# A graph attention layer on one Trainium2 core: its preparation rearranged, R copied through HBM, plain fp32 in five of eight projections

## Chip, core and metric

One of the eight cores of a Trainium2 chip. The metric is the device time of one execution in microseconds (us).

## What is computed

x is 4096 x 256 in fp32, adj a 4096 x 4096 matrix of 0 and 1 (int32), W1 is 256 x 256.

```python
h0 = jnp.maximum(_layernorm(x, axis=-1), 0.0)
h = h0 @ W1 + b1
e = jax.nn.leaky_relu((h @ a1)[:, None] + (h @ a2)[None, :] + b2, 0.2)
attention = jnp.where(adj > 0, e, jnp.float32(-1000000000000.0))
attention = jax.nn.softmax(attention, axis=1)
x = x + jax.nn.elu(attention @ h)
```

## The kernel before

The work has a preparation and a main loop. The engines have streams written out by hand, with semaphores between them; an instruction that waits holds all that stands behind it on its engine.

**Preparation.** The 32 tiles of 128 nodes go in 8 groups of 4. For a group g:

- `statistics` (VectorE): four `bn_stats`. `moments` (GpSimd): seven small steps that make mean and variance of them. `root` (ScalarE): square root. `invert` (VectorE): reciprocal and shift. `normalise`: two tiles by ScalarE, two by VectorE, into `xn`.
- `transposes` (TensorE): eight of 128 x 128 into PSUM. `relu_T` (ScalarE): relu of these into `hnT`, with row sums. `low_T` (VectorE): what the rounding to fp32r lost, into `hnT_lo`.
- `project` (TensorE): four tiles times two halves of the features, each as three fp32r matmuls (`hnT` by `W_hi`, `hnT` by `W_lo`, `hnT_lo` by `W_hi`), 258 columns. The last two columns give the two scores, h a2 and a multiple of h a1. `keep_h` (VectorE) adds the bias and writes `h_raw`, in two halves (L700).
- `exponents` (GpSimd) makes `cr`, `s2` and `cp` of the two scores. The row scores have to stand along the free dimension in every partition, as `R` (128 x 4096): `repeat_s1` (ScalarE), four transposes in `spread` (TensorE), `keep_s` (ScalarE, L374), and an exp over 1,024 columns for each chunk of rows (L378).

At the end come the sum of all h (L568, with which `h_tiny` is made), the maximum over `s2` by way of a transpose and a small matmul (L573, L575), `u` (L428), the first `hp_hi` and `hp_lo`, that is h times u in two parts.

**Main loop.** 4 chunks of 1,024 rows, in each 16 pairs of column tiles, in 4 rounds of 4 slots. For a pair: a DMA of 1 MB of adj; `sign` (ScalarE, L383); `mask` (VectorE, two instructions, L738): the larger of R and p, times the sign; `high` (ScalarE, L391) rounds to `w_hi`; `low` (VectorE, L748) writes the rest, `w_lo`; TensorE multiplies `w_hi` by `hp_hi` and `hp_lo` (32 matmuls of 258 columns, L604 and L606) and `w_lo` by `hp_hi` (16, L604) into 8 banks. In chunk 0, `scale_h`, `round_h` and `low_h` make the h of the next pairs beside that. `start_sum` puts a matmul with `h_tiny` (L580) into each bank at a chunk's start. After a chunk, ScalarE copies the banks to `y` (L455).

## Time and profile before

| | |
|---|---|
| median of 3 runs | 437.5 us (437.46 to 437.55) |
| profiled execution, its own time | 437.48 us |
| its span, first to last instruction | 435.7 us |
| TensorE busy | 412.5 us |
| VectorE busy | 377.1 us |
| ScalarE busy | 315.9 us |
| GpSimd busy | 23.0 us |
| read from HBM | 76.15 MB |

A span is shorter than the execution's own time by what lies before the first and after the last instruction. An engine counts as busy from the start of an instruction to its end, and instructions on one engine overlap a little, so that the step from one to the next is shorter than the duration of one. Each start that is named in the text is in us from the span's start.

### The profile page before, as it was taken

The page shows a single profiled execution, that of the slowest core. Times are in us where ns is not written, and L with a number is a line of the kernel's source. Part 1 is how long each engine was busy: PE and PEld are TensorE (multiplying, and loading weights), DVE is VectorE, ACT ScalarE, POOL GpSimd, SP SyncE. Part 2 cuts the span into 40 slices and gives each one's busy share as a digit, 9 for nine tenths or more (in the row PEclk, how much of TensorE's full clock was granted, in tenths as well). Part 3 has the DMA queues.
Part 4 walks back from the last instruction along what each step waited for, and adds up shares of the span by engine and source line. Part 5 has one row for each costly group of instructions (what it writes and reads, how often), then busy time and mean ns, then how long its engine had stood idle before and what let it go on. Part 6 is the DMA issues. An engine that isn't in the chain of part 4 may idle for free.

```text
span 435.7 us, 8648 instructions
## 1 busy us (share of the span) xinstructions
PE 412.5 (95%) x3399; PEld 409.1 (94%) x3399; DVE 377.1 (87%) x404; ACT 315.9 (73%) x312; POOL 23.0 (5%) x94
## 2 busy tenths in 40 slices
PE   0689979999999999999999999999999999999995
PEld 0688979999999999999999999999999999999995
DVE  3999899999999389999996299999991799999925
ACT  2678899999996298957763798859562989586512
POOL 2333200000000000000000000000000000000003
PEclk9999999999999999999999999999999999999999
DMA  8940015556555725638478155647477256476202
GB/s 271 385 178 1 0 45 211 193 213 211 193 193 194 289 93 205 235 145 261 173 254 308 68 193 200 249 152 263 154 265 259 73 219 213 174 243 238 98 0 98
DMA packets 22360, 80.68 MB, mean 185 GB/s; under 512 B 1472, under 2 KB 14016, under 8 KB 14144
## 3 DMA queue, kind: packets, MB, share of 16 engines
q1 hardware_dynamic: 21920, 79.70, 52.1%
q10 hardware_dynamic: 416, 0.66, 0.5%
q8 instruction: 16, 0.26, 0.2%
q14 instruction: 8, 0.07, 0.0%
HBM read 76.15 MB, written 4.19 MB: 184 GB/s over the span
## 4 chain that ended last, share of the span: by engine, by line
PE 88%; DVE 7%; ACT 2%; DMA 2%; issue 0%; SPq 0%; DVEq 0%; ACTq 0%
PE ps L604 51%; PE ps L606 25%; PE ps L622 2%; PE ps L623 2%; PE ps L624 2%; DVE stats L664 2%; DMA x_s<-x 2%; DVE hnT_lo L691 1%; PE ps L531 1%; DVE h_raw L700 1%; PE ps L533 1%; PE ps L532 1%; DVE xn L681 1%; PE ps L580 1%; PE ps L519 1%; ACT h_raw L439 1%
## 5 line engine op out<-in xcount | busy, mean ns | idle before, releaser
L604 PE MATMUL ps<-hp_hi,w_hi 128*128 (+1 forms) x944 | 229.8, 282 | 0.9 <-ACT w_hi L391 0.9
L606 PE MATMUL ps<-hp_lo,w_hi 128*128 (+1 forms) x944 | 229.7, 282 | 0.0
L738 DVE SCALAR_TENSOR_TENSOR adj_s<-R,p,adj_s 128x1024 f32<-128x1024 f32 x128 | 158.1, 1275 | 31.7 <-ACT adj_s L383 31.7
L604 PEld LDWEIGHTS ps<-hp_hi,w_hi 128*128 128x128 f32 x944 | 178.3, 189 | 1.2 <-ACT w_hi L391 1.1
L606 PEld LDWEIGHTS ps<-hp_lo,w_hi 128*128 128x128 f32 x944 | 178.1, 189 | 0.0
L748 DVE SCALAR_TENSOR_TENSOR w_lo<-adj_s,w_hi 128x2048 fp32r<-128x2048 f32 x64 | 146.0, 2282 | 0.4 <-ACT w_hi L391 0.3
L391 ACT ACTIVATE w_hi<-adj_s 128x2048 fp32r<-128x2048 f32 x64 | 122.4, 1912 | 29.8 <-DVE adj_s L738 29.5
L383 ACT ACTIVATE adj_s<-adj_s 128x2048 f32<-128x2048 int32 x64 | 122.3, 1912 | 23.2 <-DMA adj_s<-adj_t 23.0
L604 PE MATMUL ps<-hp_hi,w_lo 128*128 (+1 forms) x944 | 123.1, 283 | 0.6 <-DVE w_lo L748 0.6
L604 PEld LDWEIGHTS ps<-hp_hi,w_lo 128*128 128x128 f32 x944 | 117.4, 189 | 0.8 <-DVE w_lo L748 0.8
L455 ACT ACTIVATE y<-ps 128x258 f32<-128x258 f32 x24 | 9.3, 387 | 27.9 <-PE ps L624 27.9
L330 POOL TENSOR_TENSOR adj_s<-y,adj_s 128x256 f32<-128x256 f32 x7 | 4.8, 692 | 372.9 <-DVE y L886 372.9
L519 PE MATMUL ps<-ident,xn 128*128 128x128 f32 x64 | 10.2, 312 | 15.1 <-ACT xn L350 11.3
L519 PEld LDWEIGHTS ps<-ident,xn 128*128 128x128 f32 x64 | 8.5, 161 | 15.8 <-issue 11.5
L622 PE MATMUL ps<-hp_hi,w_hi 128*128 128x258 f32 x80 | 22.6, 282 | 0.0
L623 PE MATMUL ps<-hp_lo,w_hi 128*128 128x258 f32 x80 | 22.6, 282 | 0.0
L624 PE MATMUL ps<-hp_hi,w_lo 128*128 128x258 f32 x80 | 22.5, 282 | 0.0
L531 PE MATMUL ps<-W_hi,hnT 128*128 128x258 f32 x64 | 19.1, 299 | 0.8 <-DVE h_raw L700 0.6
L532 PE MATMUL ps<-W_lo,hnT 128*128 128x258 f32 x64 | 18.3, 287 | 0.0
L533 PE MATMUL ps<-W_hi,hnT_lo 128*128 128x258 f32 x64 | 18.3, 286 | 0.0
L664 DVE BATCH_NORM_STATS2 stats<-x_s 128x6 f32<-128x256 f32 x32 | 11.2, 411 | 6.0 <-DMA x_s<-x 6.0
L623 PEld LDWEIGHTS ps<-hp_lo,w_hi 128*128 128x128 f32 x80 | 15.1, 189 | 0.0
(90 smaller groups left out, 270.2 us busy)
## 6 DMA issues: line engine op xcount, KB each, us to landing
adj_s<-adj_t SPq DMA_DIRECT2D x64, 1024.0 KB, 4.8
x_s<-x SPq DMA_DIRECT2D x8, 512.0 KB, 10.4
o_s<-x SPq DMA_DIRECT2D x3, 1024.0 KB, 7.5
out<-o_s SPq DMA_DIRECT2D x6, 512.0 KB, 6.8
adj_s<-x SPq DMA_DIRECT2D x1, 1024.0 KB, 5.3
out<-adj_s SPq DMA_DIRECT2D x8, 128.0 KB, 1.7
vec<-vectors ACTq DMA_DIRECT2D x1, 384.5 KB, 6.4
W1x<-W ACTq DMA_DIRECT2D x1, 256.0 KB, 4.3
```

The lines of the kernel that those rows point to most:

```text
L383: act.activation(adj_w[:, c, :, :], adj_s[:, c, :, :], ACT.Sign).then_inc(signed, 1)
L391: act.activation(w_hi[:, c, :, :], adj_w[:, c, :, :], ACT.Relu).then_inc(hi_ready, 1)
L519: last = pe.transpose(ps[:, kc, t * P:(t + 1) * P], xn[:, u, t, kc * P:(kc + 1) * P], ident[:, :])
L531: pe.matmul(acc, hnT[:, u, kc, node], W_hi[:, kc, :], start=kc == 0, stop=False)
L532: pe.matmul(acc, hnT[:, u, kc, node], W_lo[:, kc, :], start=False, stop=False)
L604: last = pe.matmul(acc, block_w, hh, start=False, stop=False)
L606: pe.matmul(acc, block_w, hl, start=False, stop=False)
L622: pe.matmul(acc, w_hi[:, b + k, s, col], hh, start=False, stop=False)
L623: pe.matmul(acc, w_hi[:, b + k, s, col], hl, start=False, stop=False)
L624: last = pe.matmul(acc, w_lo[:, b + k, s, col], hh, start=False, stop=end)
L738: last = dve.scalar_tensor_tensor(sgn, R[:, ds(ic * CW, CW)], p[:, ds(source(r, c) + s, 1)], sgn, ALU.max, ALU.mult)
L748: dve.scalar_tensor_tensor(w_lo[:, c, :, :], adj_w[:, c, :, :], 0.0, w_hi[:, c, :, :].bitcast(fp32), ALU.max, ALU.subtract).then_inc(lo_re ...
```

## The change

- Mean and variance come from `bn_aggr` on VectorE, 32 of them; GpSimd's `moments` is gone.
- W and the vectors are loaded by the queue of x, after group 0; the first tile of adj after all of x.
- ScalarE normalises three tiles of a group from group 2 on, VectorE one. `xn` has four buffers, and the transposes take turns between two pairs of banks.
- Groups 0 to 4 are projected by plain fp32 matmuls (8 a group, no `low_T`); groups 5 to 7 as before by three products (24).
- 19 matmuls on ones stand at the start of TensorE's stream (`keep_warm`).
- `R`: `turn_r` transposes `cr` in one piece (first 8 tiles, then 24), VectorE copies it, ScalarE takes exp of the compact rows, SyncE writes them to HBM and reads them back spread over all partitions.
- The steps after the last projection take `s2` and `cr` straight from PSUM, ahead of the last `keep_h`. The matmuls with `h_tiny` move from a chunk's start to its last pair. The sum of h stands inside the last projection.
- In the first pair, `low` stands ahead of the next pair's `mask`.

```diff
-NORM_ACT = 2
+NORM_ACT = 3
+PAIRED = 2
+WARM = 19
+XN = 4
+SPLIT = 5
+R_CUT = CW // P
+R_PART = ((0, R_CUT), (R_CUT, TILES))
-EARLY = 6 * GT
+EARLY = 4 * GT
...
+            load_nodes(0)
+            sp.dma_start(W1x[:, :, 0:F], W1.rearrange("(c p) f -> p c f", p=P)).then_inc(w_in, 16)
+            sp.dma_start(vec[:, :], vectors.partition_broadcast(P)).then_inc(vec_in, 16)
+            for g in range(1, GROUPS):
                 load_nodes(g)
...
+            def spread(k):
+
+                a, b = R_PART[k]
+                tiles = slice(a, b)
+                sp.wait_ge(r_ready, k + 1)
+                sp.dma_start(r_rows[tiles, :], r_row[k][:, :]).then_inc(r_out, 16)
+                sp.wait_ge(r_out, (k + 1) * 16)
+                sp.dma_start(R[:, a * P:b * P],
+                             r_rows[tiles, :].rearrange("t p -> (t p)").partition_broadcast(P)).then_inc(R_in, 16)
...
+            def exp_r(k):
+
+                act.wait_ge(r_copied, k + 1)
+                act.activation(r_row[k][:, :], r_row[k][:, :], ACT.Exp).then_inc(r_ready, 1)
...
+            def keep_warm(n):
+
+                for _ in range(n):
+                    pe.matmul(ps[:, H0 + GT - 1, 0:P], ones[:, :], ones[:, :], start=True, stop=True)
...
+                        if g < SPLIT:
+                            last = pe.matmul(acc, hnT[:, g % 2, kc, node], W1x[:, kc, :], start=kc == 0, stop=kc == KC - 1)
+                        else:
+                            pe.matmul(acc, hnT_hi[:, g % 2, kc, node], W_hi[:, kc, :], start=kc == 0, stop=False)
+                            pe.matmul(acc, hnT_hi[:, g % 2, kc, node], W_lo[:, kc, :], start=False, stop=False)
+                            last = pe.matmul(acc, hnT_lo[kc][:, g % 2, node], W_hi[:, kc, :], start=False, stop=kc == KC - 1)
...
+            keep_warm(WARM)
             pe.wait_ge(pool_c, 3)
...
+            transposes(0)
+            pe.wait_ge(w1x_ready, 1)
+            project(0)
+            transposes(1)
+            project(1)
+            transposes(2)
+            project(2)
+            transposes(3)
+            for g in range(3, GROUPS):
+                if g + 1 < GROUPS:
+                    transposes(g + 1)
+                if g == 4:
+                    pe.wait_ge(c_ready, R_CUT // GT)
+                    pe.wait_ge(hn_ready, (g + 1) * KC)
+                    turn_r(0)
+                project(g)
+                if g == 4:
+                    pe.wait_ge(r_copied, 1)
...
                 for ib in range(BANKS):
                     acc = ps[:, ib, 0:HW].unsqueeze(1)
                     col = slice(ib * P, (ib + 1) * P)
+                    add_tiny(ib)
...
-                last.then_inc(stat_ready, 1)
+                link(last)
+                for t in range(GT):
+                    dve.bn_aggr(agg[:, g, t, :], stats[:, g, t, :]).then_inc(agg_ready, 1)
...
                 for c in range(SLOTS):
                     end = last and r is LAST_ROUND
-                    if not (end and c == SLOTS - 1):
+                    begin = first and r is FIRST_ROUND and c == 0
+                    if not (end and c == SLOTS - 1) and not begin:
                         mask(*ahead(ic, r, c, 1))
                     low(ic, r, c)
+                    if begin:
+                        mask(*ahead(ic, r, c, 1))
```

VectorE's stream around the first mask (adj_s<-R,p,adj_s) before. hnT_lo is the low part of a group, here of group 7; h_raw is what `keep_h` writes, ahead of the mask for group 6 and behind it for group 7.

```order
L691 SCALAR_TENSOR_TENSOR hnT_lo<-ps,hnT 128x512 [waits hn_ready,h_ready]
L691 SCALAR_TENSOR_TENSOR hnT_lo<-ps,hnT 128x512 [waits hn_ready]
L700 TENSOR_TENSOR h_raw<-ps,b1x 128x516 [waits h_ready] x2
L782 TENSOR_REDUCE hsum<-hs 128x2 [waits hn_ready]
L784 TENSOR_SCALAR hsrep<-ones,hsum 128x128 [waits dve_c]
L784 TENSOR_SCALAR hsrep<-ones,hsum 128x128
L738 SCALAR_TENSOR_TENSOR adj_s<-R,p,adj_s 128x1024 [waits signed,R_ready,p_ready]
L738 SCALAR_TENSOR_TENSOR adj_s<-R,p,adj_s 128x1024
L700 TENSOR_TENSOR h_raw<-ps,b1x 128x516 [waits h_ready] x2
```

The same place in the changed kernel; the first two rows are the low part of group 6, R_in is the semaphore of the DMA that brings R.

```order
L708 SCALAR_TENSOR_TENSOR hnT_lo_54<-ps,hnT_hi 128x512 [waits hn_ready,h_ready]
L708 SCALAR_TENSOR_TENSOR hnT_lo_55<-ps,hnT_hi 128x512 [waits hn_ready]
L754 SCALAR_TENSOR_TENSOR adj_s<-R,p,adj_s 128x1024 [waits signed,R_in,p_ready]
L754 SCALAR_TENSOR_TENSOR adj_s<-R,p,adj_s 128x1024
L721 TENSOR_TENSOR h_raw<-ps,b1x 128x516 [waits h_ready] x2
L708 SCALAR_TENSOR_TENSOR hnT_lo_54<-ps,hnT_hi 128x512 [waits hn_ready,h_ready]
L708 SCALAR_TENSOR_TENSOR hnT_lo_55<-ps,hnT_hi 128x512 [waits hn_ready]
```

The mask moved ahead of the `h_raw` of group 6 and of the low part of group 7, and waits for a DMA instead of for ScalarE.

VectorE's stream in the changed kernel from the last `h_raw` of the preparation into the first pairs.

```order
L721 TENSOR_TENSOR h_raw<-ps,b1x 128x516 [waits h_ready] x2
L834 MEMSET h_raw 128x4 [waits h_kept]
L835 MEMSET h_raw 128x4
L905 SCALAR_TENSOR_TENSOR hp_lo<-h_raw,u,hp_hi 128x258 [waits hp_tile] x2
L764 SCALAR_TENSOR_TENSOR w_lo<-adj_s,w_hi 128x2048 [waits hi_ready]
L754 SCALAR_TENSOR_TENSOR adj_s<-R,p,adj_s 128x1024 [waits signed]
L754 SCALAR_TENSOR_TENSOR adj_s<-R,p,adj_s 128x1024
L870 TENSOR_TENSOR hp_lo<-h_raw,hp_hi 128x516 [waits hp_pair]
```

Before, the two rows of the mask (of pair 1) stood ahead of `w_lo` (of pair 0), directly behind `hp_lo`.

ScalarE's stream in the changed kernel around the exp of r (r_row<-r_row), from the relu of group 6 on.

```order
L366 ACTIVATE hnT_hi,hs<-ps 128x512 [waits tp_ready,h_ready]
L366 ACTIVATE hnT_hi,hs<-ps 128x512 [waits tp_ready]
L372 ACT_TABLE_LOAD
L372 ACTIVATE r_row<-r_row 8x128 [waits r_copied]
L413 ACTIVATE p<-cp 128x16 [waits c_ready]
L366 ACTIVATE hnT_hi,hs<-ps 128x512 [waits tp_ready,h_ready]
```

The compact exp over 8 rows stands where the exp over 1,024 columns of R (L378) and two copies to R stood.

## Rows read from the trace of the kernel before

**Rows 1.** The page: busy us of each engine, share of the span, instructions.

```profile
PE 412.5 (95%) x3399; PEld 409.1 (94%) x3399; DVE 377.1 (87%) x404; ACT 315.9 (73%) x312; POOL 23.0 (5%) x94
```

**Rows 2.** Windows: length; busy PE, PEld, DVE, ACT, POOL; granted clock; DMA share; GB/s.

```profile
0.00:57.70 57.70, 40.40 (x301) 37.58 (x302) 46.96 (x135) 38.15 (x82) 18.17 (x87) 1.00 0.44 158
65.68:429.00 363.32, 363.32 (x3031) 363.32 (x3032) 319.07 (x254) 268.72 (x217) 2.76 (x4) 1.00 0.55 194
```

**Rows 3.** Waits of TensorE from 50 us on: us in total, times, longest.

```profile
PE ps L604 <- ACT w_hi L391: 0.9, 1, 0.9
...
PE ps L604 <- DVE w_lo L748: 0.6, 1, 0.6
```

**Rows 4.** The chain that ended last, 50 to 66 us: start, us, what.

```profile
50.91 2.39 DVE adj_s L738 x2
53.30 1.22 DVE h_raw L700 x2
...
56.13 0.33 ACT u L428
...
56.54 0.91 ACT hp_hi L433 x2
...
63.82 1.81 ACT w_hi L391
...
65.68 0.39 PE ps L604
```

**Rows 5.** Timeline of the first group: start, us of all in the row, instruction.

```profile
5.32 1.41 DVE L664 BATCH_NORM_STATS2 stats<-x_s 128x6 f32<-128x256 f32 x4 [4.37 <-DMA x_s<-x]
...
8.18 0.20 POOL L308 TENSOR_TENSOR var<-mom 128x4 f32<-128x4 f32 x1
...
9.70 0.16 DVE L671 RECIPROCAL rstd<-std 128x4 f32<-128x4 f32 x1
...
12.35 0.21 DVE L715 TENSOR_SCALAR W1x<-w1a 128x1 f32<-128x1 f32 x2
```

**Rows 6.** Timeline of TensorE: start, us of all in the row, instruction.

```profile
11.35 1.94 PE L519 MATMUL ps<-ident,xn 128*128 128x128 f32 x8 [11.35 <-ACT xn L350]
...
17.79 0.42 PE L531 MATMUL ps<-W_hi,hnT 128*128 128x258 f32 x1
...
18.52 0.28 PE L532 MATMUL ps<-W_lo,hnT 128*128 128x258 f32 x1
...
22.32 1.07 PE L519 MATMUL ps<-ident,xn 128*128 128x128 f32 x8 [1.59 <-DVE xn L681]
...
52.62 0.28 PE L533 MATMUL ps<-W_hi,hnT_lo 128*128 128x258 f32 x1
52.74 1.03 PE L568 MATMUL ps<-W1x,hsrep 128*128 128x256 f32 x4
```

**Rows 7.** Groups of instructions: busy us, mean ns of one, idle before. ACT_TABLE_LOAD likewise.

```profile
L691 DVE SCALAR_TENSOR_TENSOR hnT_lo<-ps,hnT 128x512 fp32r<-128x512 f32 x16 | 10.3, 684 | 1.8 <-ACT hnT L360 1.8
...
L360 ACT ACTIVATE hnT<-ps 128x512 fp32r<-128x512 f32 x16 | 9.3, 589 | 5.1 <-PE ps L519 5.1
...
L748 DVE SCALAR_TENSOR_TENSOR w_lo<-adj_s,w_hi 128x2048 fp32r<-128x2048 f32 x2 | 4.6, 2286 | 0.1
...
L415 ACT ACT_TABLE_LOAD x1 | 1.3, 1283 | 0.0
...
L568 PE MATMUL ps<-W1x,hsrep 128*128 128x256 f32 x4 | 1.0, 379 | 0.0
...
L455 ACT ACTIVATE y<-ps 128x258 f32<-128x258 f32 x24 | 9.3, 387 | 27.9 <-PE ps L624 27.9
```

**Rows 8.** DMA issues: number, KB each, median us to landing; x_s alone last.

```profile
adj_s<-adj_t SPq DMA_DIRECT2D x64, 1024.0 KB, 4.8
...
out<-adj_s SPq DMA_DIRECT2D x8, 128.0 KB, 1.7
...
DMA to landing us min/median/max: 4.6/10.4/12.6
```

More of the change, by code:

```diff
@@ L534, in project @@
                     if t % (GT // 2) == GT // 2 - 1:
                         last.then_inc(h_ready, 1)
-            def spread(g, u):
-                pe.wait_ge(s1_ready, g + 1)
-                if at_least(g, 2):
-                    pe.wait_ge(s_kept, g - 1)
-                for t in range(GT):
-                    last = pe.transpose(ps[:, S0 + u, t * P:(t + 1) * P], s1rep[:, u, t, :], ident[:, :])
-                last.then_inc(s_ready, 1)
-            pe.wait_ge(pool_c, 3)
-            transposes(0, 0)
@@ L564, in _, with turn_r @@
-            project(GROUPS - 1, 1)
-            pe.wait_ge(hsrep_ready, 1)
-            for kc in range(KC):
-                last = pe.matmul(ps[:, 0, 0:F], hsrep[:, kc, :], W1x[:, kc, 0:F], start=kc == 0, stop=kc == KC - 1)
-            last.then_inc(hsum_ps, 1)
-            spread(GROUPS - 2, 0)
+                    if g == GROUPS - 1 and t == 1:
+                        sum_h()
+            def turn_r(k):
+                a, b = R_PART[k]
+                pe.transpose(ps[0:b - a, RB[k], 0:P], cr[:, a:b], ident[:, :]).then_inc(rT_ready, 1)
@@ new lines, in add_tiny, with first_tile @@
+            def add_tiny(ib):
+                pe.matmul(ps[:, ib, 0:HW], ones64[:, :], h_tiny[:, :], start=False, stop=False)
+            def first_tile():
+                pe.wait_ge(hi_ready, 1)
+                pe.wait_ge(hp_tile, 1)
+                pe.wait_ge(hsum_kept, 1)
+                pe.wait_ge(r_copied, 2)
+                for ib in range(BANKS):
+                    if ib == H0:
+                        pe.wait_ge(h_kept, 2 * GROUPS)
+                    pe.matmul(ps[:, ib, 0:HW], w_hi[:, 0, 0, ib * P:(ib + 1) * P], hp_hi[:, 0, :], start=True, stop=False)
+                pe.wait_ge(hp_first, 1)
+                for ib in range(BANKS):
+                    pe.matmul(ps[:, ib, 0:HW], w_hi[:, 0, 0, ib * P:(ib + 1) * P], hp_lo[:, 0, :], start=False, stop=False)
@@ L587, in pair @@
                     for s in range(2):
+                        if first and begin and part == 0 and s == 0:
+                            first_tile()
+                            continue
                         if first and part == 0:
@@ L637, in chunk @@
                 last_pairs(ic, PAIRS - tail, SLOTS - tail, first, tail)
-            pe.wait_ge(prep_done, 1)
-            for ib in range(S0):
-                start_sum(ib)
             chunk(0, first=True)
@@ new lines, in _ @@
+            keep_h(0)
+            invert(2)
+            normalise(2)
+            statistics(3)
+            invert(3)
+            normalise(3)
+            keep_h(1)
+            statistics(4)
+            invert(4)
+            normalise(4)
+            scalars()
+            for g in range(2, GROUPS - 1):
+                if g + 3 < GROUPS:
+                    statistics(g + 3)
+                keep_h(g, (0,))
+                if g + 3 < GROUPS:
+                    invert(g + 3)
+                    normalise(g + 3)
+                if g == 4:
+                    copy_r(0)
+                if g == SPLIT - 2:
+                    split_weights()
+                keep_h(g, (1,))
+                if g + 1 >= SPLIT:
+                    low_T(g + 1)
+                if g == 5:
@@ L804, in _ @@
-            rest = slice(P // 2, P)
-            dve.wait_ge(tiny_ready, 1)
-            dve.scalar_tensor_tensor(h_tiny[rest, :], h_sum[rest, :], TINY, h_tiny[rest, :].bitcast(fp32),
-                                     ALU.mult, ALU.subtract).then_inc(prep_done, 1)
+            dve.wait_ge(hn_ready, GROUPS * KC)
+            link(dve.reduce_sum(hsum[:, :], hs[:, :, :], AX.X))
+            for kc in range(KC):
+                last = dve.tensor_scalar(hsrep[:, kc, :], ones[:, :], hsum[:, kc:kc + 1], None, ALU.mult)
```

329 lines of the change are left out of this document (144 added, 185 removed).

## Prediction

> **What bounds the kernel now.** I read the page's line of busy times first: TensorE works 95% of the span [rows 1]. Windows then split the span into two stages. From 65.68 us to 429 us TensorE is busy in every microsecond, 3,031 matmuls in 363.3 us, 0.12 us each; in the first 57.7 us it works only 40.4, and VectorE with 47.0 is the busiest [rows 2]. The waits of TensorE after 50 us are 0.9 us for `w_hi` and 0.6 us for `w_lo` in the first two pairs, and nothing later [rows 3]. So the main loop is full, and its length is fixed by its matmuls; the preparation and the first pair decide. I fix one point: the matmuls on `w_hi` of pair 1 begin at 65.68 [rows 4]. From there to the end 435.7 − 65.7 = 370.0 us pass, with no wait that an earlier delivery could shorten. The question is when that point comes in the changed kernel; call it X.
>
> The chain of work back from X [rows 4]: `w_hi` of pair 1 (ScalarE, 1.8), a queue of ScalarE work back to `u` at 56.1, the maximum over `s`, the last two `h_raw`, the first mask (2.4), and TensorE's last projection, whose last matmul starts at 52.62 and ends at 52.9 [rows 6]. Call this end E: X − E is 12.8 us before. Ahead of E, VectorE and TensorE set the pace.
>
> **The main loop.** The eight matmuls with `h_tiny` per chunk stay eight. In chunk 0 they stood before X and now stand in its last pair, behind X: 8 × 0.12 = **+0.96 us**. In the later chunks they move from the first pair to the last; a bank of the first pair now lasts 0.24 instead of 0.36 us, but seven of the eight banks are copied while the last pair runs (ScalarE waits 27.9 us in all for these banks [rows 7]), so I count nothing; without that cover a copy of 0.39 would show at each of three changes of chunk. The exp of R leaves ScalarE, which waits there already: nothing.
>
> **From E to X.** Small steps follow E: copy of `s`, maximum, transpose, maximum, matmul, copy. The same steps fill 54.5 (end of `h_raw`) to 56.1 (`u`) before, 1.6 us, and the copy is one more [rows 4]. They no longer wait for `h_raw`, which now stands behind them on VectorE: E + 1.7, then 1.3 for two `h_raw`, 0.2 for the memsets and 0.8 for two `hp_lo` (as ScalarE's `hp_hi` of the same size, 0.91) gives E + 4.0; `u` and `hp_hi`, 1.2 together on ScalarE, hide beside that. Then the new order on VectorE: first `w_lo` of pair 0 (2.2), only then the mask of pair 1 (2.4), and ScalarE's `w_hi` behind it (1.8 plus 0.1 of handing over) [rows 4, 7]. X = E + 4.0 + 2.2 + 2.4 + 2.0 = E + 10.6. Before it was 12.8, so this part gives **−2.2 us**, the moved 0.96 takes part of it back, and the change breaks even if E comes not later than 52.9 + 1.25 = 54.2.
>
> **The first group.** Its statistics end in 0.3 us on VectorE where GpSimd took 1.6 (6.7 to 8.4) [rows 5], and x is alone ahead in its queue. It lands at 5.3 now, beside W and the vectors. 128 KB take 1.7 us and 1,024 KB take 4.8 [rows 8]; the straight line gives 3.0 for 512 KB, thus 3.7 after the issue at 0.7 (5.3 less the 4.6 that this load took). I take 4.3 between 3.7 and 5.3. Then 1.4 statistics, 0.5 aggregates, 0.4 root, 0.4 inverse and shift, 1.1 for two tiles on ScalarE: transposes begin at 8.0 instead of 11.35 [rows 6]. This lead of 3.3 us is what the rest can lose.
>
> **bn_aggr** is in no row, 32 of it. The nearest rows are two tensor_scalar on one column, 0.21 together (0.06 from one to the next), and a reciprocal on four, 0.16 alone [rows 5]. I take 0.09 to the next, nearer the pipelined row; at 0.06 the sum falls by 0.6, at 0.17 it rises by 1.2.
>
> **Projection in plain fp32.** L568 is a plain matmul of 256 columns; the program has two, the trace four records, spread over 1.03 us with a last one of 0.38: 0.217 from one to the next, 0.43 a matmul [rows 6, 7]. A group has eight: 3.46 us. The split form has 24 at 0.12: 2.88. So TensorE pays 0.58 more in each of five groups, and VectorE is spared 2 × 0.6 for `hnT_lo` in each [rows 7]. The chain relu, low part, matmul also loses one link. The Trainium skill (FP8 and Floating Point Precision, TensorE Precision Notes) says true fp32 takes four passes through the array, thus 4 × 0.12 = 0.48 where the row gives 0.43. By the page the sum would be 0.9 higher, and I keep the row.
>
> **Group by group, up to E.** `transposes(g+1)` stands behind `project(g)` for the first groups, so TensorE, ScalarE and TensorE follow one another. A turn is: eight transposes 0.9 (eight take 1.07 with the last one's end [rows 6]), two relus of which 1.1 lies behind them (0.59 each [rows 7]), projection 3.5. Transposes 8.0, projection 0 at 10.1 to 13.5, projection 1 at 15.6 to 19.1. Root 3 stands on ScalarE behind relu 2 (end 21.0), and VectorE, done with statistics 3 at 18.1, stands waiting for it with `h_raw` of group 1 queued behind; it comes at 22.5, and projection 2 needs that bank: 22.6 to 26.1. Projection 3 waits for `h_raw` of group 2, which stands behind statistics 5: 29.5 to 33.0. Projection 4 runs 34.0 to 37.5. Then TensorE waits for the copy of r, queued behind root 8 and normalise 7: 39.1. Transposes 6, the low part of group 5 (1.3), and projection 5 is 40.9 to 43.9; transposes 7, low part 6 behind two `h_raw`, projection 6 from 46.0 to 48.9. TensorE is idle for some 12 us of this, so the saved work on VectorE turns into waits, and the lead of 3.3 is used up at about here.
>
> **R by DMA.** ScalarE gives 16 steps away (eight s1rep, eight copies to R, over 512 columns like the relu, 0.6 each), TensorE 32 transposes. In their place r goes to HBM and comes back. ScalarE finishes relu 6 at 41.3, loads the table (1.28 [rows 7]) and takes exp: 42.7. The write is 4 KB: 1.3 by the line, 1.7 as for 128 KB, 3.0 if it costs what 512 KB cost; I take 1.75, by the nearest row. The read of 512 KB: 3.0 by the line, 4.6 as the quickest x [rows 8]; nothing else is under way, so nearer the line, 3.4. R lands at 42.7 + 1.75 + 3.4 = 47.9. VectorE has been waiting with the first mask since 45.9, and **behind it stand `h_raw` 6 and the low part of group 7**, on which the last projection hangs. Mask 2.4, h_raw 1.2, low part 1.3: 52.8. Projection 7 with the sum of h inside it: 24 × 0.12 + 2 × 0.43 = 3.75, and its tail 0.25: **E = 56.8**.
>
> **Sum.** X = 56.8 + 10.6 = 67.4. Span = 67.4 + 370.0 + 0.96 = 438.4, against 435.7: **+2.7 us**. The profiled execution took 437.48, 1.8 more than its span and as long as the median of 437.5. Forecast: 437.5 + 2.7 = **440.2 us**, slower by 0.6%. A change under 0.2%, 0.9 us, cannot be told from none.
>
> **The rivals.**
> *R is there in time* (chance 0.12). The two transfers take under 3.2 us together and the mask does not wait. E falls by up to 2.0 and the time to 438.2 to 438.9: within or just beyond what can be told. Against it: no transfer in the profile lands in under 1.7, and half a megabyte has taken 4.6 at the least.
>
> *The lead holds* (faster; chance 0.08). It decides on TensorE between 8.0 and E. Its work there is 8 × 0.9 + 5 × 3.46 + 3 × 2.88 + 0.86 = 34.0 us, so that 14.8 us of the 48.8 are waits. If these waits are 3.6 us shorter, E comes before 53.2 and the kernel is faster; if the lead of 3.3 stays whole, E is 49.6 and the time 433.0 us. For it speaks that 6.5 us of `hnT_lo` and a quarter of the normalising leave VectorE, the bound of that stage. Against it: the order of the code puts a wait for another engine into each turn.
>
> *The clock falls* (chance 0.22). TensorE's eight transposes take 1.94 us at 11.35 and 1.07 at 22.3, and a matmul lasts 0.42 at 17.8 and 0.28 at 18.5 [rows 6]: 1.2 GHz, then 2.4, though the granted clock reads 1.00 [rows 2]. It rose under steady work, after two bursts of transposes. Nineteen plain matmuls on 128 columns now come first, 0.22 each at the upper level (half of 0.43) and 0.43 at the lower: 4 to 8 us from 0.95 on. I take 7.2 and a raised clock at 8.0; all at the lower level would put the transposes at 9.2. But for R TensorE stands idle from 48.9 to 52.8, longer than the 1.6 ahead of 22.3, which the upper level outlasted. Projection 7 at the lower level costs 2.9 to 3.7 more: 443 to 444 us. Lost already in group 0 and 1, it costs 1.5 to 3.5: 442 to 444. The Trainium skill (TensorE: Matmul & The Clock Gate, Why this matters for your kernels) also warns that idle gaps between matmul bursts bring the lower clock back; no row here shows a fall.
>
> **How the numbers follow.** The sum as it stands, 0.58: its bounds are −0.6 and +1.0 for x, −0.6 and +1.2 for bn_aggr, −0.8 and +2.5 for R; not all at one end they make 439.0 to 442.2. With R in time 438.2, with a lost clock 444. Leaving out the lead and the worst of the clock, the range is 438.3 to 444.0. Slower by over 0.2%: 0.58 + 0.22 + a part of R in time = 0.82; same 0.10; faster 0.08.
>
> **What would show it.** Right: transposes near 8.0; plain matmuls in two records of 0.22; a wait of VectorE on the DMA of R ahead of the first mask, about 2 us, and one of TensorE of nearly 4 us ahead of the last projection; E near 56.8; about 2 us of waiting for `w_hi` of pair 1, at 67.4; no wait later. Wrong: transposes after 9; E before 54; R landed before the mask; matmuls 0.24 apart after 8 us; TensorE waiting in the later rounds or where chunks meet.

## The result and the profile after

The changed kernel takes 442.86 us (median of 4 runs, 441.27 to 444.19), against 437.52 us (437.46 to 437.68, 4 runs) on the same chip: ratio 1.012, 95% interval 1.010 to 1.0139. It is slower by 5.3 us; 440.2 was forecast. The profiled execution is the quickest of the four, 441.27 us with a span of 439.3, at a mean granted clock of 0.995. The other three have 0.991 and take 1.3 to 2.9 us more: times that agreed to 0.2 us before now scatter over 2.9.

The page of the changed kernel has, for busy times, the line that answers to [rows 1].

```profile
PE 417.3 (95%) x3367; PEld 411.4 (94%) x3367; DVE 372.4 (85%) x423; ACT 308.8 (70%) x300; POOL 10.6 (2%) x39
```

VectorE, ScalarE and GpSimd all work less than before, and the kernel is longer. Windows show where (columns as in [rows 2]); the last is the stretch from the start of `w_hi` of pair 1, the point X, to 432 us.

```profile
41.50:46.50 5.00, 4.52 (x25) 4.55 (x26) 0.92 (x2) 2.38 (x7) 0.00 (x0) 0.66 0.07 27
46.50:68.50 22.00, 14.85 (x113) 13.59 (x111) 17.43 (x33) 13.88 (x22) 1.51 (x7) 1.00 0.35 132
68.50:432.00 363.50, 363.49 (x3034) 363.49 (x3035) 320.14 (x256) 266.70 (x213) 2.75 (x4) 1.00 0.55 193
```

From X on TensorE is full as before. Ahead of it TensorE stands idle for 7.15 of the 22 us, and in the window of 41.5 the granted clock reads 0.66. TensorE's waits of the whole execution (us in total, times, longest):

```profile
PE ps L532 <- DVE hnT_lo L708: 4.4, 3, 2.2
PE ps L530 <- DVE h_raw L721: 3.7, 2, 2.6
PE ps L530 <- DVE W1x L736: 1.8, 1, 1.8
PE ps L621 <- ACT w_hi L385: 1.6, 1, 1.6
PE ps L594 <- ACT hp_hi L424: 1.4, 1, 1.4
PE ps L514 <- DVE r_row L771: 1.2, 1, 1.2
```

TensorE's timeline (start, us of all in the row, in brackets the idle time ahead and its releaser) has the preparation, with projections 0, 2 and 3 in plain fp32:

```profile
1.00 6.27 PE L503 MATMUL ps<-ones 128*128 128x128 f32 x38 [1.00 <-POOL ones L312]
8.11 1.07 PE L514 MATMUL ps<-ident,xn 128*128 128x128 f32 x8 [0.84 <-ACT xn L356]
10.96 3.75 PE L530 MATMUL ps<-W1x,hnT 128*128 128x258 f32 x16 [1.79 <-DVE W1x L736]
...
23.78 3.73 PE L530 MATMUL ps<-W1x,hnT 128*128 128x258 f32 x16 [2.59 <-DVE h_raw L721]
...
30.61 3.73 PE L530 MATMUL ps<-W1x,hnT 128*128 128x258 f32 x16 [1.14 <-DVE h_raw L721]
...
41.98 0.36 PE L532 MATMUL ps<-W_hi,hnT_hi 128*128 128x258 f32 x1 [0.90 <-DVE hnT_lo L708]
...
42.30 0.42 PE L534 MATMUL ps<-W_hi,hnT_lo 128*128 128x258 f32 x1
42.52 0.42 PE L532 MATMUL ps<-W_hi,hnT_hi 128*128 128x258 f32 x1
...
48.80 0.35 PE L532 MATMUL ps<-W_hi,hnT_hi 128*128 128x258 f32 x1 [1.30 <-DVE hnT_lo L708]
...
54.11 0.36 PE L532 MATMUL ps<-W_hi,hnT_hi 128*128 128x258 f32 x1 [2.18 <-DVE hnT_lo L708]
```

The first transposes are at the upper level and at the time forecast (8.0). Projection 0 waits for `W1x`, which waits for the vectors. Inside projection 5 the matmuls go over from 0.12 to 0.215 us apart and last 0.42 each, as in the row at 17.79 of [rows 6]: 1.2 GHz, until 45.7.

VectorE's timeline says why TensorE waits:

```profile
5.70 0.38 DVE L683 BATCH_NORM_AGGREGATE agg<-stats 128x2 f32<-128x6 f32 x4
...
22.33 0.18 DVE L689 RECIPROCAL rstd<-std 128x4 f32<-128x4 f32 x1 [3.08 <-ACT std L347]
...
22.95 1.28 DVE L721 TENSOR_TENSOR h_raw<-ps,b1x 128x516 f32<-128x516 f32 x2
...
47.27 1.28 DVE L708 SCALAR_TENSOR_TENSOR hnT_lo<-ps,hnT_hi 128x512 fp32r<-128x512 f32 x2
48.50 2.48 DVE L754 SCALAR_TENSOR_TENSOR adj_s<-R,p,adj_s 128x1024 f32<-128x1024 f32 x2
50.89 0.69 DVE L721 TENSOR_TENSOR h_raw<-ps,b1x 128x516 f32<-128x516 f32 x1
51.97 0.69 DVE L721 TENSOR_TENSOR h_raw<-ps,b1x 128x516 f32<-128x516 f32 x1 [0.38 <-PE ps L534]
52.58 1.28 DVE L708 SCALAR_TENSOR_TENSOR hnT_lo<-ps,hnT_hi 128x512 fp32r<-128x512 f32 x2
```

VectorE stands idle 3.08 us for the root of group 3, with `h_raw` of group 1 ready to be written behind it, and projection 2 hangs on that. And between 48.50 and 53.8 it works through mask, two `h_raw` and the low part of group 7, in this order, while TensorE waits for the last of them. It stands idle for 0.38 us of this, ahead of the second `h_raw`, until projection 6 has ended. No bracket stands at the mask: in this execution R was there in time. The chain that ended last (start, us, what) has R and the way to X:

```profile
43.83 1.22 DMA r_rows<-r_row
45.07 2.88 DMA R<-r_rows
...
58.14 0.16 DVE s L821
...
59.82 0.33 ACT u L419
60.24 0.91 ACT hp_hi L424 x2
...
66.61 1.86 ACT w_hi L385
68.52 0.39 PE ps L621
```

The chain's 2.88 for the read of R ends at 47.95, where the chain goes on with a low part of VectorE; it isn't the transfer's own length. From issue to landing the list of DMA issues has 3.3 us:

```profile
R<-r_rows SPq DMA_DIRECT2D x1, 512.0 KB, 3.3
```

So R lands at 45.07 + 3.3 = 48.4, 0.1 us before the mask starts. The last projection ends at 58.1 (E), and X is 68.52: X − E is 10.4.

### The profile page after: what moved, and what is told of

Same layout as the page of the kernel before. It is cut to its first block, busy times and chain, and to the rows that moved or that the text cites. A ratio compares the mean times of both kernels' runs of the same rounds, so it can differ in the third digit from the quotient of the medians.

```text
span 439.3 us, 8507 instructions
## 1 busy us (share of the span) xinstructions
PE 417.3 (95%) x3367; PEld 411.4 (94%) x3367; DVE 372.4 (85%) x423; ACT 308.8 (70%) x300; POOL 10.6 (2%) x39
## 4 chain that ended last, share of the span: by engine, by line
PE 87%; ACT 5%; DVE 4%; DMA 3%; issue 1%; SPq 0%; ACTq 0%; DVEq 0%
PE ps L621 51%; PE ps L623 25%; PE ps L643 2%; PE ps L641 2%; PE ps L642 2%; PE ps L530 2%; DMA vec<-vectors 2%; DVE stats L680 1%; PE ps L583 1%; ACT adj_s L377 1%; DVE h_raw L721 1%; DMA R<-r_rows 1%; ACT hnT L366 1%; ACT h_raw L430 1%; PE ps L532 1%
## 5 line engine op out<-in xcount | busy, mean ns | idle before, releaser
L621 PE MATMUL ps<-hp_hi,w_hi 128*128 (+1 forms) x936 | 226.8, 282 | 1.6 <-ACT w_hi L385 1.6
L623 PE MATMUL ps<-hp_lo,w_hi 128*128 (+1 forms) x936 | 226.8, 282 | 0.0
L621 PEld LDWEIGHTS ps<-hp_hi,w_hi 128*128 128x128 f32 x936 | 176.8, 189 | 1.8 <-ACT w_hi L385 1.8
L764 DVE SCALAR_TENSOR_TENSOR w_lo<-adj_s,w_hi 128x2048 fp32r<-128x2048 f32 x64 | 146.1, 2284 | 0.0
L621 PEld LDWEIGHTS ps<-hp_hi,w_lo 128*128 128x128 f32 x944 | 117.3, 189 | 0.0
L530 PE MATMUL ps<-W1x,hnT 128*128 128x258 f32 x80 | 18.6, 385 | 6.4 <-DVE h_raw L721 3.7
L530 PEld LDWEIGHTS ps<-W1x,hnT 128*128 128x128 f32 x80 | 14.8, 189 | 9.4 <-issue 4.2
L641 PEld LDWEIGHTS ps<-hp_hi,w_hi 128*128 128x128 f32 x80 | 15.1, 189 | 0.0
L643 PEld LDWEIGHTS ps<-hp_hi,w_lo 128*128 128x128 f32 x80 | 15.0, 188 | 0.0
L496 ACT ACTIVATE y<-ps,rden 128x256 f32<-128x256 f32 x8 | 3.8, 476 | 15.4 <-DVE rden L917 15.4
L721 DVE TENSOR_TENSOR h_raw<-ps,b1x 128x516 f32<-128x516 f32 x16 | 10.6, 680 | 4.6 <-PE ps L534 4.6
L356 ACT ACTIVATE xn<-x_s,shift,rstd 128x256 f32<-128x256 f32 x22 | 11.7, 591 | 3.9 <-DVE shift L690 3.9
```

What stands on the lines that cost most here:

```text
L356: last = act.activation(xn[:, g % XN, t, :], x_s[:, tile, :], ACT.Identity, scale=rstd[:, tile:tile + 1], bias=shift[:, tile:tile + 1])
L530: last = pe.matmul(acc, hnT[:, g % 2, kc, node], W1x[:, kc, :], start=kc == 0, stop=kc == KC - 1)
L621: last = pe.matmul(acc, block_w, hh, start=fresh, stop=False)
L623: pe.matmul(acc, block_w, hl, start=False, stop=False)
L641: pe.matmul(acc, w_hi[:, b + k, s, col], hh, start=False, stop=False)
L643: last = pe.matmul(acc, w_lo[:, b + k, s, col], hh, start=False, stop=end)
```

## The experiments

Each is the changed kernel with one edit, unless it says otherwise, and its ratio is to the kernel before on the same chip (437.44 to 437.57 us). The changed kernel has 1.012 (1.010 to 1.0139), from four executions that scatter by 2.9 us. A variant whose interval overlaps this one isn't told from it by its median; there only the traces speak, and each of them shows one execution.

### Is it the clock, and the idle time before it?

Three kernels touch what TensorE does while it would stand idle. The first puts matmuls on ones into the pauses behind the transposes of group 2, behind projection 4 and ahead of projections 5 to 7; of its edit, the last three are shown.

```diff
+            def fill(bank, count):
+                for _ in range(count):
+                    pe.matmul(ps[:, bank, 0:P], ones[:, :], ones[:, :], start=True, stop=True)
...
+                if g >= SPLIT:
+                    pe.wait_ge(h_kept, 2 * g - 1)
+                    fill(H0, (4, 5, 8)[g - SPLIT])
```

> The changed kernel with plain 128-column matmuls on ones put into TensorE's pauses: 9 behind the transposes of group 2, 5 behind projection 4, and 4, 5 and 8 ahead of projections 5, 6 and 7; nothing else is changed. Theory (the time above the sum of 440.2, and the scatter of 441.3 to 444.2 from run to run, are falls of TensorE's clock in the pauses of the preparation; the profiled run had one, from 42.3 to 45.7 us): no matmul between 8 and 430 us is at 0.22, projection 5 takes 2.9 instead of 4.5 us, the median falls by 1.5 to 3 us to 440 to 441.3, and the runs lie within 0.5 us of each other. Rival (the scatter comes from DMA landings or from somewhere later, the fall costs nothing since ScalarE and the round trip of R set the pace there): the median stays within 0.8 us of 442.9 and the scatter stays; or it rises by up to 2 us, as the added matmuls stand in the way.

Measured: 441.35 us (440.63 to 445.61, 6 runs), ratio 1.0109 (1.0077 to 1.0141). In its trace projections 5 to 7 run 0.12 apart throughout. The low level comes later, in the first pair of the main loop (61.4 to 64.6), where TensorE's slower work takes the place of a wait for `w_hi` that it has otherwise. The run with the highest granted clock, 0.999, took 440.63, and the one with the lowest, 0.987, 445.61. Here the times go with the clock, which makes it the likely cause of the scatter. But the theory asked for no fall and for runs within 0.5 us, and they lie 5.0 apart; the median is 1.5 lower, which the intervals don't tell from nothing. What the clock costs the changed kernel isn't settled by this. The run at 0.999, with hardly a fall, is still 3.2 us slower than the kernel before. And now VectorE's timeline shows the wait for R (here the mask is L764):

```profile
48.28 2.48 DVE L764 SCALAR_TENSOR_TENSOR adj_s<-R,p,adj_s 128x1024 f32<-128x1024 f32 x2 [1.52 <-issue]
```

The view names no releaser. But the read of R was issued at 44.78 and took 3.4 us to land, thus 48.2, and in all six variants that show such a wait the mask starts about 0.1 us behind R's landing. The mask begins at 48.28 in place of 48.50. The fall in projection 5 of the changed kernel cost it little by itself: it lay beside the wait for R, and hid it.

The second takes the warming away.

```diff
-WARM = 19
+WARM = 0
```

> The changed kernel without the 19 matmuls on ones. Theory (they put TensorE at the upper level before group 0): transposes of group 0 take 1.94 us and projection 0 runs at 0.43 a record for at least its first 3 us; projection 0 ends 1.5 to 3.5 us later, all of it stays in the chain of the preparation, time 1.5 to 3.5 us more. Rival (W1x comes at 10.9 anyway, and the level rises within projection 0): under 1 us.

Measured: 445.05 us (443.86 to 445.95, 5 runs), ratio 1.0166 (1.0152 to 1.018), 2.2 us more than with it. TensorE's timeline:

```profile
8.32 1.94 PE L514 MATMUL ps<-ident,xn 128*128 128x128 f32 x8 [8.32 <-ACT xn L356]
11.13 5.72 PE L530 MATMUL ps<-W1x,hnT 128*128 128x258 f32 x16 [0.87 <-ACT hnT L366]
...
56.47 0.55 PE L532 MATMUL ps<-W_hi,hnT_hi 128*128 128x258 f32 x1 [3.37 <-DVE hnT_lo L708]
```

Transposes 0 take 1.94 and projection 0 takes 5.72 instead of 3.75: the warming pays in this kernel, as the theory had it. The third puts the same 19 matmuls at the start of the kernel before, and changes nothing else there.

```diff
+            for _ in range(19):
+                pe.matmul(ps[:, H0 + GT - 1, 0:P], ones[:, :], ones[:, :], start=True, stop=True)
```

> The kernel before with the 19 matmuls on ones at the start of TensorE's stream and nothing else. Theory (before the change VectorE sets the pace of the preparation, so a faster TensorE in the first groups is worth little): transposes and projection 0 at the upper level, the median within 0.6 us of 437.5. Rival (the clock is worth what it is in the changed kernel): 1 us or more faster.

Measured: 437.54 us (437.42 to 437.58 in 11 of 12 runs; the twelfth took 2,299.23 us, which nothing here explains, and is left out of the ratio), ratio 0.9999 (0.9991 to 1.0008). Its transposes of group 0 are no faster than in [rows 6]:

```profile
0.98 7.45 PE L548 MATMUL ps<-ones 128*128 128x128 f32 x38 [0.98 <-POOL ones L285]
11.33 1.94 PE L519 MATMUL ps<-ident,xn 128*128 128x128 f32 x8 [2.90 <-ACT xn L350]
```

The pause of 2.90 us behind the warming has lost the upper level again (the granted clock is 0.93 from 8 to 11 us and 0.50 from 11 to 14); in the changed kernel it is 0.84, and the level holds. The time is as forecast, but the theory isn't tested by it: its transposes and the start of projection 0 never ran at the upper level.

### What is late: R, the mask, or the low part?

The mask one group later, so that `h_raw` 6 and the low part of group 7 don't stand behind it:

```diff
-                if g == 5:
+                if g == 6:
                     dve.wait_ge(p_ready, 1)
                     dve.wait_ge(R_in, 16)
                     mask(0, 0, 0)
```

> The changed kernel with the first mask moved on VectorE behind the low part of group 7 and the h_raw of group 6. Theory (the first mask, 2.4 us, stands in the chain of the last projection, with or without a wait for R): projection 7 starts right behind projection 6, its last matmul ends about 2.2 us earlier (55.9 instead of 58.1 in the profile), and as the first w_hi (51 to 53) still comes long before it is needed, the time falls by 1.5 to 2.3 us. Rival (the first pair needs the mask early, so that the delay of w_hi takes back what the projection wins; or ScalarE is late with relu 7): the time falls by less than 0.7 us. The scatter from the clock stays in both.

Measured: 442.11 us (441.2 to 446.04, 6 runs), ratio 1.0138 (1.0105 to 1.0171). The gain of 1.5 to 2.3 us did not come. The low part of group 7 still stands behind both `h_raw` of group 6 and runs at 51.12, and TensorE's wait for it remains as it was: projection 7 starts 5.31 us after projection 6 here (52.65 against 47.34) and in the changed kernel's trace (54.11 against 48.80). So in that trace the mask delayed nothing; it filled time in which the second `h_raw` would have waited for projection 6. The mask now stands ahead of the sum of h, for which TensorE waits inside the last projection.

```profile
PE ps L532 <- DVE hnT_lo L708: 4.4, 3, 2.2
PE ps L530 <- DVE h_raw L721: 2.6, 1, 2.6
...
PE ps L549 <- DVE hsrep L813: 1.1, 1, 1.1
```

With the mask in its place and projection 5 at the upper level, it does delay: in the run of the section on the first pair, projection 7 starts 6.47 us after projection 6 (53.66 against 47.19), 1.2 later, and then runs at the lower level.

The low part is now to go ahead of both `h_raw`, and the mask behind the sum of h:

```diff
-                keep_h(g, (0,))
+                if g >= SPLIT:
+                    low_T(g + 1)
+                else:
+                    keep_h(g, (0,))
...
-                if g == 5:
-                    dve.wait_ge(p_ready, 1)
-                    dve.wait_ge(R_in, 16)
-                    mask(0, 0, 0)
...
             last.then_inc(hsrep_ready, 1)
+            dve.wait_ge(p_ready, 1)
+            dve.wait_ge(R_in, 16)
+            mask(0, 0, 0)
```

> The changed kernel with VectorE's order of the kernel before for groups 5 to 7: the low part of group g+1 ahead of both h_raw of group g, and the first mask behind the replicated sum of h, so ahead of nothing that projection 7 needs. Theory (VectorE's order costs more than the DMA of R: TensorE waits 0.9, 1.3 and 2.2 us ahead of projections 5, 6 and 7 for the low part, which stands behind h_raw and the mask): the waits ahead of 6 and 7 vanish, with about 1 us more from projection 5's follow-on, the last projection ends 4 to 5 us earlier (near 53.5 instead of 58.1) and the median falls by 4 to 5.5 us to 437.4 to 438.9. Rival (TensorE's clock decides, the pauses only move): the time falls by under 2.5 us. Second rival (R by DMA decides): the mask waits for R at 47.9 to 48, ends at 50.4, so w_hi of pair 0 is there at 52.4 and costs nothing; if it costs, the wait ahead of the first main matmul is longer than the 1.4 us of now.

Measured: **436.27 us** (435.99 to 436.71, 7 runs), ratio 0.9971 (0.996 to 0.9982), 6.6 us below the changed kernel. VectorE's timeline of this kernel:

```profile
46.68 1.29 DVE L708 SCALAR_TENSOR_TENSOR hnT_lo<-ps,hnT_hi 128x512 fp32r<-128x512 f32 x2 [0.59 <-ACT hnT_hi L366]
47.89 0.68 DVE L721 TENSOR_TENSOR h_raw<-ps,b1x 128x516 f32<-128x516 f32 x1
...
50.37 2.47 DVE L754 SCALAR_TENSOR_TENSOR adj_s<-R,p,adj_s 128x1024 f32<-128x1024 f32 x2
```

The low part of group 7 runs at 46.68 instead of 52.58. No wait of TensorE is left between projections 5 and 7, E is 53.1, and the mask finds R there: its read was issued at 45.30 and took 4.0 us, and the mask begins 1.1 us after it landed. The scatter is down to 0.7 us. The gain is above the 4 to 5.5 us of the theory. By the two traces E comes 5.0 us earlier: 3.5 are the waits ahead of projections 6 and 7, which are gone, and 1.5 the fall of the clock in projection 5, which didn't come. The edit moves two things, and as the mask alone brought nothing clear of the noise, the waits go to the low part behind `h_raw`; the low part alone wasn't run. Projection 2 ran at the lower level in this execution, 5.41 us instead of 3.73, behind the same pause of 2.59. Most of this was made good by the wait of 1.14 us ahead of projection 3, which was gone: from the start of projection 2 to that of projection 4 it is 11.83 us instead of 11.38.

### The first pair

`low` of pair 0 behind the mask of pair 1 again, as before the change:

```diff
-                    if not (end and c == SLOTS - 1) and not begin:
+                    if not (end and c == SLOTS - 1):
                         mask(*ahead(ic, r, c, 1))
                     low(ic, r, c)
-                    if begin:
-                        mask(*ahead(ic, r, c, 1))
```

> The changed kernel with the order of the kernel before in the first pair: the mask of pair 1 ahead of the low part of pair 0. Theory A, as in the prediction (w_hi of pair 1 waits for the mask behind w_lo): the wait of 1.6 us for w_hi of pair 1 shrinks by 1 us or more and the time falls by 1 us. Theory B, from the profile of the changed kernel (ScalarE is busy without a gap from 59.8 until w_hi of pair 1 starts at 66.55, so the mask that ends at 66.5 is late by nothing): the start of w_hi stays, w_lo of pair 0 comes 2.4 us later, TensorE waits before it instead, in sum less than 0.3 us either way.

Measured: 442.59 us (441.86 to 443.09, 4 runs), ratio 1.012 (1.0105 to 1.0134), no different from the changed kernel. The wait for `w_hi` of pair 1 is gone, and one of the same length for `w_lo` of pair 0 is there, as theory B had it. The 3.3 us are the wait ahead of projection 7, where VectorE's mask had waited 1.59 us:

```profile
PE ps L532 <- DVE hnT_lo L708: 5.5, 3, 3.3
...
PE ps L621 <- DVE w_lo L764: 1.6, 1, 1.6
```

### The front

W and the vectors by ScalarE's queue, instead of behind x of group 0 in SyncE's:

```diff
-            sp.dma_start(W1x[:, :, 0:F], W1.rearrange("(c p) f -> p c f", p=P)).then_inc(w_in, 16)
-            sp.dma_start(vec[:, :], vectors.partition_broadcast(P)).then_inc(vec_in, 16)
...
+            act.dma_start(W1x[:, :, 0:F], W1.rearrange("(c p) f -> p c f", p=P)).then_inc(w_in, 16)
+            act.dma_start(vec[:, :], vectors.partition_broadcast(P)).then_inc(vec_in, 16)
```

> The changed kernel with W and the vectors loaded by ScalarE's queue again, as before the change. Theory (projection 0 waited 1.8 us for W1x because the vectors landed only at 8.9 behind W in one queue, and this shifts the whole preparation): W1x is ready 1.0 to 1.3 us earlier, but x lands at 5.3 instead of 4.3 and the transposes start 1 us later; projection 0 starts at about 11.0 to 11.3 as now, time within 0.6 us of the changed kernel. Rival (one of the two loads alone is what counts): if W1x alone counts, 0.9 to 1.2 us faster; if x alone counts, 1.0 us slower.

Measured: 444.33 us (442.96 to 447.05, 5 runs), ratio 1.0152 (1.0139 to 1.0165), 1.5 us worse by the medians, more than the theory's 0.6 and with intervals that just touch. The profiled execution is the slowest of the five, 447.05, so its falls aren't those of the median. In it the transposes of group 0 begin at 9.38 behind a pause of 2.47 us, and projection 0 then takes 6.77 us, at the lower level for most of it. x of group 0 now lands at 5.53 instead of 4.26, and the vectors are ready only 0.25 us earlier (8.72 against 8.97). Projection 0 starts at 11.46 instead of 10.96. In trying to save the 0.9 us that `W1x` costs, x was made late, and in this execution the clock was lost.

Two swaps at the place where VectorE waits 3.08 us for the root:

```diff
             statistics(3)
+            keep_h(1)
             invert(3)
             normalise(3)
-            keep_h(1)
...
-            relu_T(2)
             root(3)
+            relu_T(2)
             normalise(3)
```

> Two places of the changed kernel are swapped and nothing else: VectorE writes h_raw of group 1 ahead of the inverse and shift of group 3, and ScalarE takes the root of group 3 ahead of the relu of group 2. Theory A (order): the 2.59 us that TensorE waits ahead of projection 2 come from h_raw of group 1, which stands on VectorE behind the inverse of group 3, which waits 3.08 us for the root, which stands behind relu 2. Then that wait shrinks from 2.59 to under 0.8, projection 2 begins near 22, R and the last projections come some 2 us earlier, and the time is 440.4 us (439.5 to 441.5) against 442.9. Theory B (data): the later stages are set by something else, above all by the low part of group 7 behind h_raw of group 6 and by the clock in projections 5 to 7; then the wait ahead of projection 2 shrinks but the ones ahead of projections 6 and 7 grow, and the time stays at 442 to 443.

Measured: 439.9 us (438.39 to 442.77, 7 runs), ratio 1.0059 (1.0038 to 1.008): 3.0 us below the changed kernel. This is within theory A. The profiled execution, though, is one of the two longest (442.70): in it projection 0 ran at the lower level, 5.44 us instead of 3.75, behind waits of only 1.16 and 1.30 us. Projection 2 starts behind 0.98 us of waiting instead of 2.59, projection 3 behind 0.41 instead of 1.14. The mask still stands ahead of the low part and waits 1.69 us for R, and TensorE waits 3.45 us ahead of projection 7, which then runs at the lower level. So the trace shows the waits in front go, and what theory B says of the later ones as well; no trace shows one of the executions near 439.9.

```profile
29.30 3.73 PE L530 MATMUL ps<-W1x,hnT 128*128 128x258 f32 x16 [0.41 <-DVE h_raw L721]
...
52.66 0.55 PE L532 MATMUL ps<-W_hi,hnT_hi 128*128 128x258 f32 x1 [3.45 <-DVE hnT_lo L708]
```

Both together, the low part first and the two swaps:

> The two swaps at the front (h_raw of group 1 ahead of the inverse of group 3, root of group 3 ahead of relu of group 2) together with the order of the run before (low part of the next group ahead of both h_raw for groups 5 to 7, first mask behind the sum of h), which alone measured 436.27. Theory A (both lie on one path, one after the other): the last projection ends 1 to 2.6 us earlier again, near 51.5, and the time is 434.5 us (433.8 to 435.6), below both kernels. Theory B (ScalarE is the bound by now): w_hi of pair 1 stands on ScalarE behind its own queue, and the copy of r and root 8 keep their places, so that what is gained in front turns into waits ahead of the transposes of group 6 or for w_hi; the time is 435.8 to 436.4.

Measured: **433.25 us** (433.16 to 434.32, 5 runs), ratio 0.9908 (0.9896 to 0.9921). This is below both kernels, and below theory A's range: 4.3 us below the one before, 9.6 below the changed one. TensorE's timeline (the last row is the last matmul of projection 7):

```profile
21.72 3.75 PE L530 MATMUL ps<-W1x,hnT 128*128 128x258 f32 x16 [0.98 <-ACT hnT L366]
...
27.64 3.73 PE L530 MATMUL ps<-W1x,hnT 128*128 128x258 f32 x16 [0.41 <-DVE h_raw L721]
...
37.11 1.09 PE L514 MATMUL ps<-ident,xn 128*128 128x128 f32 x8 [1.27 <-DVE r_row L771]
...
49.68 0.28 PE L534 MATMUL ps<-W_hi,hnT_lo 128*128 128x258 f32 x1
```

E is 49.96. On top of it, VectorE's copy of r ahead of the statistics of group 7, to take away the 1.27 ahead of the transposes of group 6:

```diff
             for g in range(2, GROUPS - 1):
+                if g == 4:
+                    copy_r(0)
                 if g + 3 < GROUPS:
                     statistics(g + 3)
...
-                if g == 4:
-                    copy_r(0)
```

> As the run with both changes of order, and VectorE's first copy of r stands ahead of the statistics of group 7 instead of behind the normalising of that group. If the wait of 1.2 to 1.6 us ahead of the transposes of group 6 (TensorE waits for the copy of r, which stands behind normalise 7) lies on the path, it goes and the time falls by another 0.2 to 1.2 us below that run (433.3 to 434.3 if that one takes 434.5). If the wait only moves, to the low part or the xn of group 7 which come later by the copy, nothing changes within 0.2%.

Measured: 434.81 us (432.91 to 436.42, 6 runs), ratio 0.9931 (0.9909 to 0.9953). The wait moves: nothing ahead of the transposes, 2.21 us ahead of projection 5, for ScalarE's relu. By the medians this is worse than the version before it, but in the profiled execution `W1x` came later (a wait of 2.29 instead of 1.27) and projection 0 ran at the lower level; the run with granted clock 0.999 is the quickest seen here, 432.91. That the copy of r gains nothing, or up to 0.3 us, is all that it shows.

### Is splitting the last three groups worth it?

All eight groups in plain fp32, once in the changed kernel and once in the best version:

```diff
-SPLIT = 5
+SPLIT = 8
```

> The changed kernel with all eight projections in plain fp32 (the boundary 5 moved to 8); W is still split, but not used. Theory (a plain projection costs TensorE 0.58 us more, but the wait for the low part, 4.4 us in sum, goes; the first mask stays in front of h_raw 6, which projection 7 waits for): projections 5 to 7 take 3.5 us each, one wait of 2.5 to 3 us remains ahead of projection 7, and the time falls by 0.3 to 1.2 us. Rival (plain fp32 costs what its passes cost, 3 x 0.58): 1.7 us slower. Rival (TensorE works more densely, so the clock falls less): over 1.5 us faster and less scatter.

> The version with both changes of order (433.25 us), with groups 5 to 7 in plain fp32 as well, so that no low part is left. Theory A (TensorE sets the pace of these groups once the order is right: it waits only 0.9 us ahead of projection 5 and not at all ahead of 6 and 7): three projections cost 0.58 us more each, the wait of 0.9 goes, and the time rises by 0.8 to 1.7 us to 434.1 to 435.0. Theory B (VectorE sets it, busy 15.3 of the 16 us after 46 us): it is spared 3 x 2.5 = 7.5 us... of which only the part ahead of the last projection counts, 2.5 us, and the time falls to 431 to 433. If the clock alone decides, it falls back at another place and the runs scatter by over 2 us.

Measured: 440.7 us (440.25 to 441.24, 5 runs), ratio 1.0074 (1.0061 to 1.0087), for the first, 2.2 below the changed kernel; 433.4 us (433.06 to 433.53, 4 runs), ratio 0.9904 (0.9888 to 0.9921), for the second, the same as with the split. In the order of the changed kernel the low parts are what TensorE waits for, so leaving them out pays. It pays more than the theory's 0.3 to 1.2, and the runs scatter by 1.0 instead of 2.9 us, which is what the rival with the clock foretold; but in the trace projection 7 falls to the lower level here too, behind a wait of 2.95, so how much is order and how much clock isn't separated. In the better order they are ready in time; plain fp32 begins 1.1 us earlier (38.01 against 39.10, no low part ahead of projection 5) and needs 0.5 more in each group, and E moves by 0.4, to 50.4. In the first pair a wait of 1.6 us for `w_hi` then stands where the best version has its stretch at the lower clock (54 to 57 us). Neither of the two theories of the second run held: neither TensorE's 0.8 to 1.7 more nor VectorE's relief shows in the time.

## Why the forecast was right in its sign and short in its size

The change was forecast to cost 2.7 us and cost 5.3.

**The main loop** held. From X to the end the span has 439.3 − 68.5 = 370.8 us, against 370.0 + 0.96 forecast, and no wait stands in it. **From E to X** held: 10.4 against 10.6. What I took for VectorE's chain is ScalarE's as well: it works without a gap from 59.8 to X. The experiment with the mask first shows what the order of `low` and mask is worth, nothing, as whichever comes second is waited for 1.6 us.

**The first group** held (transposes 8.1), and so did `bn_aggr`: four take 0.38, under 0.10 from one to the next, against 0.09. **Plain fp32** held: projections of 3.75 with the last one's end, where the sum had 3.46 without that end. Without it the eight matmuls of a group take 3.59: the transposes of the next group begin that much after the projection (14.55 against 10.96). The Trainium skill (FP8 and Floating Point Precision, TensorE Precision Notes) has true fp32 as four passes through the array; at 0.12 a pass, an estimate, the group would take 3.84. The row doesn't bear out the 0.12: if there are four passes, one takes 0.11. That they would have added 0.9 to the sum has no working in the prediction; eight matmuls at 0.05 more are 0.4 a group.

**The landing of W and the vectors** was left out of the sum. I timed x by its size and let projection 0 follow the relus; it waited 1.79 us for `W1x` and began at 10.96 instead of 10.1. This delay stays, as 0.9 to 1.2 us, to projection 5 (41.98 against 40.9). That it comes from the vectors is read from one trace; the run that loads them by another queue moved x as well and doesn't separate it.

**R by DMA** landed 0.5 us later than forecast, at 48.4 instead of 47.9: the exp ended 1.1 later, at 43.8, the write took 1.22 where I had 1.75, and the read 3.3 where I had 3.4. The wait of the mask, forecast at 2 us, isn't there in the profiled execution, and by the prediction's own signs "R landed before the mask" stood for wrong. It landed 0.1 us before it, since the slow projection 5 had delayed the low part of group 6 by 1.6. In five variants with the same three products the wait is 1.52 to 1.85 us, so the step exists, but it isn't what held this trace back. There the last projection waited 2.18 us, and not nearly 4, and this wait is as long when the mask stands elsewhere. What the centre of the forecast, "mask, `h_raw` 6, low part, projection 7", had right is the low part at its end: put ahead of both `h_raw`, with the mask moved as well, it is worth 6.6 us. From mask to projection 7 it took 5.6 us and not 4.9: `h_raw` of group 6 had to wait for a projection 6 that was late itself. E came at 58.1 instead of 56.8, and that it came so near is in part luck: a fall of the clock stood where the wait for R had been forecast.

**The clock** was priced as a rival and stood in the sum at nothing. Together with E this is what the sum had too small. The profiled run of 441.27 is 1.1 over the forecast, of which E gives 1.3. The median is 1.6 above that run. It lies where the rival with the clock had put the time, at 442 to 444 with a chance of 0.22, and above the 439.0 to 442.2 of the sum with its bounds. The granted clock is 0.995 in the quickest run and 0.991 in the others. As an estimate, the fall from 42.3 to 45.7 takes half of 3.4 us out of 439, 0.004; so 0.991 stands for one more fall of such a length. Where it lies in these untraced runs, and that it makes their 1.6 us, is not shown: with the mask one group later, a run at 0.990 took 441.20 and one at 0.995 441.69.

What a fall costs depends on what stands behind it. Ahead of projection 7, TensorE's pause was 2.95 to 3.61 us in five kernels, and in all five the projection then ran at the lower level; it was 2.2 in the changed kernel and with the mask late, and there it did not. In the four of them with three products it then lasted 5.4 to 6.8 us instead of 4.0, thus 1.4 to 2.8 more, and all of it moves E; the rival had charged 2.9 to 3.7 for a projection 7 that is slow from end to end. Behind the pause of 2.59 ahead of projection 2 the clock fell in four kernels and held in three. That projection then lasted 1.4 to 1.7 more, but projection 4 began only 0.2 to 0.5 later, as the wait ahead of projection 3 was gone. In projection 0 it fell in three warmed kernels, behind waits of 1.16 and 1.30, of 0.38 and 2.29, and of 2.47 and 1.01 us. In the first pair of the main loop a fall costs little, since TensorE would otherwise wait for `w_hi`. The Trainium skill (TensorE: Matmul & The Clock Gate, Why this matters for your kernels) warns of idle gaps between matmul bursts. The traces agree, but the clock also fell behind shorter ones, as in projection 5 behind waits of 1.18 and 0.90 us.

**The rival that the lead holds** gave 433.0 us at E = 49.6. The version with the two changes of order has E = 49.96 and takes 433.25. So its arithmetic was right, and so was the reason against it: the order of the code turned the lead into waits. Nothing that the change adds or removes had to go for this; a few statements had to stand elsewhere.

## What to carry to other kernels

When work is taken off the engine that bounds a stage, redo the order of what remains: ask for each instruction that others wait for what stands ahead of it in its queue, and whether that itself waits. Here the low part ahead of both `h_raw`, with the mask behind the sum of h, brought 6.6 us, and an `h_raw` ahead of an inverse that waits for a root of a later group, with that root moved forward, 3.0. A mask that waits for a DMA round trip is better off behind what TensorE needs next. In this kernel the level of the clock fell behind every wait of TensorE of 2.95 us or more ahead of projection 7, and where no later wait took it up, that cost 1.4 to 2.8 us more. Times that begin to scatter can be a sign of it: look at the granted clock of the runs before comparing medians.

## What the runs showed of the hardware that was not expected

- Whether a pause of 2.59 us brings the lower level differed between seven kernels whose streams are nearly the same up to there (four fell, three held), so that one profile doesn't tell a kernel's clock.
- The upper level that 19 matmuls on ones had raised survived a pause of 0.84 us and was gone after one of 2.90. After one of 2.47 the transposes still ran at it (1.07 us), and projection 0, 1.01 us later, fell.
- Writing 4 KB to HBM took 1.22 us, less than any transfer in the profile of before. The 512 KB read back and spread over the partitions took 3.3 to 4.0 in the twelve kernels that do it, not clearly less than the quickest x of the same size in the changed kernel, 3.5.
